# Expert stage of a perceiver layer: TensorE takes the expert pairs two at a time by kind of product, and 15 further tiles' weights are gathered by row

## The reference

```python
x = x + xattn(layernorm(x), ctx)      # 16 heads, 8192 keys, rotary positions
x = x + attn(layernorm(x))            # causal, 16 heads, rotary positions
x = x + ffn(layernorm(x))

def ffn(x):                           # T = 512, D = 512, E = 32 experts, H = 128, TOPK = 4
    scores = softmax(x @ router_w.T + router_bias)
    topk_scores, topk_idx = top_k(scores, 4)
    topk_scores = topk_scores / clip(topk_scores.sum(-1), 1e-12)
    h = silu(einsum('nd,ehd->neh', x, gate_w)) * einsum('nd,ehd->neh', x, up_w)
    expert_out = einsum('neh,edh->ned', h, down_w)
    out = (take(expert_out, topk_idx) * topk_scores[..., None]).sum(1)
    return out + (silu(x @ sgate_w.T) * (x @ sup_w.T)) @ sdown_w.T   # shared, 512 wide
```

## Time and profile before

| | us |
|---|---|
| median of 3 runs (lowest, highest) | 1469.47 (1468.87, 1470.29) |
| the profiled execution | 1470.23 |
| its span (first to last instruction) | 1468.6 |

### The profile page before, as it was taken

The page is one execution under the profiler, slowest core; times in us unless marked ns, Lnnn a source line. Parts: engine busy times, 40 slices in busy tenths (PEclk is TensorE's granted clock), DMA queues, the critical chain, the costliest instruction groups (busy, mean ns, idle before and its releaser), DMA issues.

```text
span 1468.6 us, 29139 instructions
## 1 busy us (share of the span) xinstructions
PE 1416.1 (96%) x11048; PEld 859.0 (58%) x11048; DVE 1149.3 (78%) x2815; ACT 1027.1 (70%) x1328; POOL 616.9 (42%) x413
## 2 busy tenths in 40 slices
PE   7999999999999987899999999999999999999998
PEld 5866666666666654455555555555555676654443
DVE  6888777777787786699999989998999777653333
ACT  5477777777777775798988998988999736411221
POOL 0199797877787992113222223220000303024541
PEclk9999999999999998899999999999999999999999
DMA  5464334443433305864545454545643330078994
GB/s 197 137 241 162 130 130 149 149 157 137 156 130 130 130 30 164 230 161 123 124 120 124 117 139 111 125 118 137 177 117 95 112 151 1 29 280 331 410 408 190
DMA packets 93809, 229.76 MB, mean 156 GB/s; under 512 B 11826, under 2 KB 12347, under 8 KB 90855
## 3 DMA queue, kind: packets, MB, share of 16 engines
q1 hardware_dynamic: 88016, 218.40, 46.9%
q0 software_dynamic: 5088, 8.41, 1.6%
q10 hardware_dynamic: 566, 1.09, 0.2%
HBM read 171.20 MB, written 64.88 MB: 161 GB/s over the span
## 4 chain that ended last, share of the span: by engine, by line
PE 75%; POOL 9%; DVE 7%; issue 3%; ACT 3%; DMA 1%; SPq 0%; POOLq 0%; DVEq 0%; ACTq 0%
PE PS L818 18%; PE PS L842 16%; PE PS L345 8%; PE PS L341 8%; PE PS L300 5%; PE PS L1701 4%; PE PS L1722 2%; PE PS L1635 2%; PE PS L850 2%; POOL W_ L632 2%; POOL kr L631 2%; POOL kr L634 2%; POOL R L623 1%; POOL kl L649 1%; DVE rel L608 1%
## 5 line engine op out<-in xcount | busy, mean ns | idle before, releaser
L876 ACT ACTIVATE P<-PS 128x1024 f32<-128x1024 f32 x512 | 487.3, 1026 | 63.4 <-PE PS L818 58.2
L608 DVE CUSTOM_DVE_ANT_0 rel<-PS,rel 128x256 f32<-128x256 f32 x1024 | 363.2, 421 | 110.9 <-PE PS L300 107.7
L936 DVE TENSOR_TENSOR W_<-W_,P 128x2048 f32<-128x2048 f32 x108 | 254.8, 2425 | 8.4 <-ACT P L876 8.1
L842 PE MATMUL PS<-P,qe 128*32 128x256 f32 (+1 forms) x4032 | 255.8, 386 | 0.0
L936 DVE TENSOR_TENSOR acc<-acc,P 128x2048 f32<-128x2048 f32 x108 | 245.3, 2335 | 12.8 <-ACT P L876 12.5
L842 PEld LDWEIGHTS PS<-P,qe 128*32 128x32 f32 x4032 | 115.5, 109 | 115.8 <-issue 54.5
L460 ACT ACTIVATE rel<-PS 128x1024 f32<-128x1024 f32 x128 | 131.7, 1029 | 72.2 <-PE PS L300 71.8
L345 PE MATMUL PS<-Wh,R 128*128 128x512 f32 x512 | 181.8, 418 | 0.0
L341 PE MATMUL PS<-R,Wh 128*128 128x512 f32 x512 | 175.6, 414 | 3.6 <-ACT kr L427 3.6
L466 ACT ACTIVATE rel<-PS 128x1024 f32<-128x1024 f32 x128 | 131.6, 1028 | 47.8 <-PE PS L300 47.3
L300 PE MATMUL PS<-khd,qh 32*128 32x256 f32 x2048 | 131.2, 329 | 24.5 <-DVE mpart L608 11.3
(11 more groups left out here) (325 smaller groups left out, 2064.2 us busy)
## 6 DMA issues: line engine op xcount, KB each, us to landing
khd<-kscr SPq DMA_DIRECT2D x129, 256.0 KB, 4.2
y<-in_y SPq DMA_DIRECT2D x16, 1024.0 KB, 5.2
vscr<-W_ SPq DMA_DIRECT2D x16, 1024.0 KB, 4.9
kscr<-khd SPq DMA_DIRECT2D x16, 1024.0 KB, 7.1
kscr<-kl SPq DMA_DIRECT2D x16, 1024.0 KB, 5.1
qe<-vscr SPq DMA_DIRECT2D x64, 256.0 KB, 2.7
kl<-kscr SPq DMA_DIRECT2D x63, 256.0 KB, 4.0
Wq<-in_w_e SPq DMA_DIRECT2D x12, 768.0 KB
```

The source lines that it names most:

```text
L608: last = dve.tensor_tensor_reduce(out=rel[i][:, j, t, :], in0=PS[:, 2 * b + j, t * 256:(t + 1) * 256], in1=rel[i][:, j, t, :], scale=1.0, ...
L842: ins = pe.matmul(PS[32 * hd:32 * hd + 32, 6, cols], vt[n % 3][:, j, 32 * hd:32 * hd + 32], P[z % 4][:, hd, cols], start=kt == 0, stop=kt ...
L876: act.activation(P[s % 4][:, 2 * pr:2 * pr + 2, :], PS[:, 2 * b:2 * b + 2, :], ACT.Exp, scale=SCALE).then_inc(exp_done, 1)
L936: dve.tensor_tensor(a[:, :, :], a[:, :, :], P[s % 4][:, :, :], ALU.add).then_inc(summed, 1)
```

## The change

Three things are done in the last stage.

1. **Two pairs together.** PE's loop steps by two: hidden of pairs i-3 and i-2, tokens of i+2 and i+3, down of i-3 and i-2, gate and up of i and i+1. DVE, ACT and POOL follow the same rotation. There are 4 `xsT` instead of 2 and 3 `h` instead of 2, and to make room 4 `xs` instead of 6.
2. **Gathered weights.** Loads 26 to 33, that is the further tiles k = 16 to 30, are no longer issued by SP but by POOL, each tile as an indirect DMA that gathers 128 rows of 6144 B by `w_rows` = 128 owner + partition. They are issued when the slot is free and behind the stores of that step on POOL; from load 28 on POOL first waits until load n-2 has landed (`gathered[n % 2]`).
3. **None without owner.** For a tile without owner all 128 indices are past the bound of 4095, so its gather moves nothing; `w_expert` no longer stands for it.

```diff
-NXS = 6
+NXS = 4
+GATHERED = 26
+GATHERED_AFTER = {freed_by(n): n for n in range(GATHERED, 34)}
-    xsT = [sbm(f"xsT{i}", [128, 4, 128]) for i in range(2)]
+    xsT = [sbm(f"xsT{i}", [128, 4, 128]) for i in range(4)]
-    h = [sbm(f"h{i}", [128, 128]) for i in range(2)]
+    h = [sbm(f"h{i}", [128, 128]) for i in range(3)]
...
-        pe.wait_ge(pair_in[SLOT[n]], landed(n))
+        if n < GATHERED:
+            pe.wait_ge(pair_in[SLOT[n]], landed(n))
+        else:
+            pe.wait_ge(gathered[n % 2], got(n))
...
         turn_tokens(0)
+        turn_tokens(1)
         shared_down(2)
-        for i in range(PAIRS + 2):
-            if i + 1 < PAIRS:
-                turn_tokens(i + 1)
-            if i < PAIRS:
-                pair_products(i)
-            if 0 < i <= PAIRS:
-                turn_hidden(i - 1)
-            if i > 1:
-                pair_down(i - 2)
+        for i in range(0, PAIRS + 2, 2):
+            older = [z for z in (i - 3, i - 2) if z >= 0]
+            for z in older:
+                turn_hidden(z)
+            for z in (i + 2, i + 3):
+                if z < PAIRS:
+                    turn_tokens(z)
+            for z in older:
+                pair_down(z)
+            for z in (i, i + 1):
+                if z < PAIRS:
+                    pair_products(z)
+        turn_hidden(PAIRS - 1)
+        pair_down(PAIRS - 1)
         last_part()
...
+        dve.scalar_tensor_tensor(w_rows[:, :], owner[:, :], 128.0, cst[:, 21:22].to_broadcast([128, 31]),
+                                 ALU.mult, ALU.add).then_inc(shares4, 1)
...
-        for i in range(PAIRS + 1):
...
+        for i in range(0, PAIRS + 2, 2):
+            for z in (i - 3, i - 2):
+                if z >= 0:
+                    keep_turned(z)
+            for z in (i + 2, i + 3):
+                if z < PAIRS:
+                    empty_tokens(z)
+            for z in (i, i + 1):
+                if z < PAIRS:
+                    gate_hidden(z)
...
+    def gather_weights(n):
+        pool.wait_ge(shares4, 13)
+        pool.wait_ge(out_made, freed_by(n) - 1)
+        if n - 2 >= GATHERED:
+            pool.wait_ge(gathered[n % 2], got(n - 2))
+        for b in halves(n - 2):
+            k = 2 * (n - 18) + b
+            pool.indirect_dma_start(weights(n, b), None, A["w_e"].rearrange("e p n -> (e p) n"),
+                                    bass.IndirectOffsetOnAxis(ap=w_rows[:, k:k + 1], axis=0),
+                                    bounds_check=4095, oob_is_err=False).then_inc(gathered[n % 2], 16)
...
-        for i in range(PAIRS + 2):
-            if i + NXS < PAIRS:
-                fetch_tokens(i + NXS)
-            if i > 1:
-                store_outputs(i - 2)
+        for i in range(-2, PAIRS + 2, 2):
+            for z in (i + 2 + NXS, i + 3 + NXS):
+                if z < PAIRS:
+                    fetch_tokens(z)
+            for z in (i - 3, i - 2):
+                if z >= 0:
+                    store_outputs(z)
+            for z in (i - 3, i - 2):
+                if load_of(z) in GATHERED_AFTER:
+                    gather_weights(GATHERED_AFTER[load_of(z)])
+        store_outputs(PAIRS - 1)
...
-        for n in range(11, 34):
+        for n in range(11, GATHERED):
...
+        sp.wait_ge(out_made, freed_by(33) - 1)
         load(sp, weights(33, 1), A["w_e"][35]).then_inc(pair_in[SLOT[33]], 16)
```

More of the change, by code:

```diff
@@ L140, in landed @@
 def landed(n):
-    return sum(16 if k < 18 else 32 for k in range(n + 1) if SLOT[k] == SLOT[n])
+    return sum(16 if k < 18 else 32 for k in range(min(n + 1, GATHERED)) if SLOT[k] == SLOT[n]) + 16 * (n == 33)
 def freed_by(n):
     return slot_use(n)[1]
+GATHERED = 26
+GATHERED_AFTER = {freed_by(n): n for n in range(GATHERED, 34)}
 def halves(i):
@@ L1570, in program @@
     w_expert = sbm("w_expert", [128, 31], I32)
+    w_rows = sbm("w_rows", [128, 31], I32)
     cmp_ = sbm("cmp", [128, 1024])
@@ L1605, in load_of, with got @@
         return 2 + i
+    def got(n):
+        return sum(16 * len(halves(k - 2)) for k in range(GATHERED, n + 1) if k % 2 == n % 2)
     x_kept, x_out = sem("x_kept"), sem("x_out")
+    gathered = [sem(f"gathered{i}") for i in range(2)]
     xs_in = [sem(f"xs_in{i}") for i in range(NXS)]
@@ L1711, in turn_hidden @@
             pe.wait_ge(x_done, i + 1)
-        pe.transpose(PS[:, i % 2, 0:r], h[i % 2][0:r, :], ident[0:r, 0:r]).then_inc(h_turned, 1)
+        pe.transpose(PS[:, i % 2, 0:r], h[i % 3][0:r, :], ident[0:r, 0:r]).then_inc(h_turned, 1)
     def pair_down(i):
@@ L1766, in fourth_act @@
             act.activation(sgs[:, :], PS[:, SHARED[e][0], :], ACT.Silu).then_inc(silu_done, 1)
-        for i in range(PAIRS + 2):
-            if i < PAIRS:
-                r = 64 * len(halves(i))
-                act.wait_ge(gu_made, 6 + i + 1)
-                if i > 1:
[L1772 to L1780, removed]
+        for i in range(0, PAIRS + 2, 2):
+            for z in (i - 3, i - 2):
+                if z >= 0:
+                    keep_output(z)
+            for z in (i, i + 1):
+                if z < PAIRS:
+                    silu(z)
             if i == 8:
@@ L1787, in fourth_act, with silu, keep_output @@
         act.activation(sgs[:, :], PS[:, SHARED[3][0], :], ACT.Silu).then_inc(silu_done, 1)
+    def silu(i):
+        r = 64 * len(halves(i))
+        act.wait_ge(gu_made, 6 + i + 1)
+        if i > 1:
+            act.wait_ge(h_made, 3 + i - 1)
+        act.activation(sg[i % 2][0:r, :], PS[0:r, 4 + i % 2, 0:128], ACT.Silu).then_inc(silu_done, 1)
+    def keep_output(z):
+        r = 64 * len(halves(z))
+        act.wait_ge(out_made, z + 1)
+        if z >= NO:
+            act.wait_ge(o_out[z % NO], 16 * (z // NO))
+        act.copy(O[z % NO][0:r, :], PS[0:r, 2 + z % 2, :]).then_inc(o_done, 1)
     def of_tokens(a):
@@ L1938, in fourth_dve @@
         empty_tokens(0)
+        empty_tokens(1)
         dve.wait_ge(shared_out, 3)
@@ L1941, in fourth_dve @@
             dve.tensor_tensor(X[:, t, :], X[:, t, :], PS[:, t, :], ALU.add).then_inc(x_done, 1)
-        for i in range(PAIRS + 1):
[L1943 to L1958, removed]
+        for i in range(0, PAIRS + 2, 2):
+            for z in (i - 3, i - 2):
[4 more added lines that the diff above has]
+                    empty_tokens(z)
+            for z in (i, i + 1):
+                if z < PAIRS:
+                    gate_hidden(z)
+        keep_turned(PAIRS - 1)
         shared_hidden(3)
```

22 lines of the change are left out of this document (18 added, 4 removed).

## The result

| | us |
|---|---|
| the kernel before, median of 4 runs | 1469.88 (1468.87 to 1471.33) |
| the changed kernel, median of 4 runs | 1485.80 (1485.57 to 1489.80) |
| ratio | 1.0113, interval 1.0097 to 1.013 |
| profiled execution of the changed kernel, its span | 1489.8, 1488.5 |

What follows compares the result with a forecast made beforehand. The prediction took PE's chain to bound the kernel, with the DMAs full too: 1470.2 - 13.2 (PE alone) + 8.2 (wait for weights) = 1465.2 us profiled, 1464.4 as a median, range 1457.5 to 1470.5.

Steps and rivals of the forecast that it cites:

- POOL: POOL's queue in the last stage: a gather costs 1.3 us (bounds 1.2 and 3.9), leaving POOL 2 us from being the bound.
- Do the new orders add waits?: Copies before PE's down products: almost no added waits, about 0.3 and 0.9 us in the last two rounds only.
- What bounds: Last stage before the change: PE's chain of 3.74 us a pair, with DMAs also full but 14.5 us ahead.
- What the pairing removes: PE's changes between kinds of product: two instead of eight in two pairs, so 6.55 us instead of 7.47.
- hidden by 0.2 us: DVE's copy of hidden i-3, behind the gating of i-1: ready near +1.1, before PE reaches down at about +1.3.
- What the DMAs give back: Weights up to pair 25 land at 1409.5; loads 26 and 27 overtake, so PE loses about 8.2 us at pairs 21 to 23.
- the slow rival: POOL ends last: a gather costs 3 us or more, owner or not, giving +9 us, 1478.6; chance 0.11.
- The sum: Whole kernel: 1470.2 - 13.2 gained on PE + 8.2 waiting for weights = 1465.2 profiled, 1464.4 as a median.
- Slower: Outcome above the "same" band of 1466.5 to 1472.4 us: chance 0.12, from 0.11 + 0.01.

Runs made afterwards that it cites:

- f4: The kernel before, without the loads of the tiles k = 20 to 30 (left out by number); 1469.19 us, ratio 0.9998.
- g1: e2 with the two hidden copies on DVE put ahead of the gating of a round's second pair; 1463.53 us, ratio 0.9957.
- f2: The changed kernel with the eleven ownerless gathers replaced on POOL by memsets of about the same length; 1469.02 us, ratio 0.9994.
- e3: The changed kernel without the eleven ownerless gathers, loads 26 and 27 still gathered; 1468.18 us, ratio 1.0002.
- e1: Pairing alone: the changed kernel's rotation, but SP issues every load as in the kernel before, ownerless tiles too; 1468.26 us, ratio 0.9995.
- e2: Pairing with all weights loaded by SP and no loads for tiles k = 20 to 30 (left out by number); 1461.77 us, ratio 0.9957.
- f1: e2 with POOL held until PE's hidden turns of the round, then issuing fetches and then stores; 1475.97 us, ratio 1.0048.
- g3: g1 with each round's two stores issued a round later, at the round's start, and the token fetches behind them; 1492.01 us, ratio 1.014.
- f3: The kernel before's one-pair rotation, with POOL gathering loads 26 to 33 behind its stores and 4 xs; 1489.18 us, ratio 1.0137.

## Why the prediction was wrong

Two terms were put at nothing and were not. The decisive one is in "POOL": a gather was given a price only in POOL's own time, and none on PE's path, where eleven empty ones cost about 16 us. The other is in "Do the new orders add waits?": the 0.2 us by which a copy was hidden held only for reports that come on time. Then the one wait that the sum did have, 8.2 us for weights, did not come.

**What bounds.** Right for the kernel before: PE, with the DMAs full behind it. f4 (weights relieved, nothing gained) shows it.

**What the pairing removes.** Right in size: 6.56 us a round where no report is late, the down to gate and up boundary free, PE busy for 105.2 us of g1's pair loop (forecast 1432.5 - 1327.8 = 104.7). Wrong in "hidden by 0.2 us": that margin of the copy of hidden i-3 behind the gating of i-1 was worked out with a silu 0.2 us behind the products. In the changed kernel, from the second round on and up to 1440, the silu of the second pair came 0.2 to 3.7 us later than that, and in nearly every round this went onto the path. The row with the silu on time was of a store with 1.2 us of pause ahead of it: POOL was issuing (1366.82 to 1367.84), but not the third or fourth DMA in a row.

**What the DMAs give back.** The wait failed as put. The landing was right (by the changed kernel's queue 23.56 of 23.60 MB were in by 1410 and 23.59 by 1411, forecast 1409), but no wait of 8.2 us followed, for PE was already later than that. It waited 1.1 us at L1715 in all, at 1431.6 and 1432.3, and not at pairs 21 to 23.

**POOL.** This is the step that failed. Right in its price: 1.29 to 1.35 us from start to start, owner or not. Wrong in what the price buys. I had POOL's time as the only way in which a gather could cost, so 1.3 us, under the 2.05 from which the slow rival decides, made it harmless. f2 shows that POOL's time costs nothing and that the issuing costs 16 to 17.5 us (e3, f2): eleven gathers that move nothing, 1.5 to 1.6 us each on PE's path. The slower rival had the right sign and about the right place, and the wrong mechanism: at 1.31 us a gather it costs nothing.

**The sum.** Forecast -13.2 + 8.2. The runs, taken apart by ratios: pairing -0.7 (e1, within its interval of nothing, for the weights bind); no loads without owner -5.6 (e2 against e1); gathers for loads 26 and 27 +6.6 (e3 against e2); eleven empty gathers +16.3. The steps lie end to end, so that they add up to the 16.6 us of the ratio 1.0113 (15.9 by the medians) is no check of them. The pair loop shows the same from PE's side, first g1, then the changed kernel:

```profile
1324.94:1437.12 112.18, 105.18 (x776) 60.26 (x775) 35.17 (x97) 29.16 (x71) 56.89 (x56) 1.00 0.79 304
```
```profile
1329.13:1465.60 136.47, 115.60 (x776) 63.72 (x775) 35.61 (x97) 28.94 (x71) 71.98 (x71) 0.91 0.65 250
```

Of the 24.3 us more, 13.9 are idle time (20.9 against 7.0) and 10.4 are the same products at a lower clock (0.91 against 1.00). So a microsecond of pause cost 1.75 in all: the rest is the slow stretch behind it. e3 shows it too (0.83 in 1380 to 1400, with a pause of 3.3 us), and e1 behind its wait of 2.05; g1, with three waits of 1.8 to 2.05, kept 1.00 from 1340 to 1440.

**Chances.** "Slower" had 0.12, all for one mechanism of POOL's time. No rival asked whether the reports of the other engines still arrive on time when POOL issues more DMAs, though the trace of before could have been searched for it. It would have told little: there POOL's DMAs come two at a time with a pause behind, and one silu of 32 is late, by 0.36 us.

**Left open.** Why PE's updates and not those of ACT and DVE are held, and by what in the chip; whether it is the issue of a DMA that holds them or what it sets off. That they pass about once in each POOL DMA is my reading of the semaphore records at 1420 to 1430; no run varied the spacing of the DMAs. Nor was a kernel found that has both the fetches early enough and POOL quiet at the round's end. The best is e2, level with g1: pairs together, every load by SP, none for tiles without owner, 0.4% faster than before.

## What to carry to other kernels

Count the DMAs that GpSimd issues in one row, not only the time they take: two with a pause behind cost nothing here, four on end made a report of TensorE up to 2.5 us late (e2), six to twelve made pieces of 3 to 8 us on the path, even if they move no byte. Leave a transfer out rather than issue an empty one, and let SyncE issue what it can. Where a rotation leaves a margin of 0.2 us, look for what can make its producer late, and put the operation that others wait for ahead of the one that may be late.

## What the runs showed of the hardware

- From the start of the last product step to the silu on ACT it is 0.43 us in a quiet moment, and beside memsets on POOL (f2); it was 4.10 while POOL issued six indirect DMAs in a row (silu at 1392.30) and 6.29 in the row of twelve and behind it. PE's update itself is recorded late (1392.27 for a product that ended at 1388.57).
- A single indirect DMA on POOL during the last product step does not delay it: 0.42 to 0.43 us in 31 of 32 pairs of the kernel before.
- An indirect DMA whose indices are all out of bounds costs POOL 0.99 to 1.04 us, one that moves 786 KB 1.01 to 1.05.
- A fetch of 128 rows of 2 KB took 8.4 us (f1) and 7.2 (g3) from its issue to its landing, and 13 behind gathered weights on its own queue (f3).
- TensorE's granted clock fell to a mean of 0.80 over 20 us in which PE was busy for 12; behind a pause of 2.95 us eight records of down took 3.68 us instead of 1.87.
